# A decoder layer's projected keys: one copy out of PSUM as f32, both f16 halves made from that copy in SBUF

## What is computed

```python
q = qdq(x) @ qdq(wq).T + bq                    # 56 x 256 per batch, 16 heads of 16
kv = cond @ wkv.T + bkv                        # cond: 1500 x 256 per batch
k, v = jnp.split(kv, 2, axis=-1)
attn = softmax(einsum('bnhd,bmhd->bhnm', q, k) * scale)
o = einsum('bhnm,bmhd->bnhd', attn, v)
```

## Time and profile before

| what | value |
|---|---|
| median of 3 runs | 856.81 us (855.29 to 857.29) |
| the profiled execution | 855.01 us, of which 853.2 us are the span shown |
| TensorE busy | 772.5 us, 91% of the span |
| VectorE busy | 638.0 us, 75% |
| ScalarE busy | 510.9 us, 60% |
| GpSimd busy | 296.4 us, 35% |

### The profile page before, as it was taken

The page is one execution under the profiler, slowest core; times in us unless marked ns, Lnnn a source line. Parts: engine busy times, 40 slices in busy tenths (PEclk is TensorE's granted clock), DMA queues, the critical chain, the costliest instruction groups (busy, mean ns, idle before and its releaser), DMA issues.

```text
span 853.2 us, 30042 instructions
## 1 busy us (share of the span) xinstructions
PE 772.5 (91%) x12379; PEld 582.2 (68%) x12379; DVE 638.0 (75%) x1234; ACT 510.9 (60%) x1084; POOL 296.4 (35%) x366
## 2 busy tenths in 40 slices
PE   4689989999998999999899999999897799999996
PEld 2356666566666666666666666666665589999995
DVE  5877667777787879778787878877774735688887
ACT  2346666566576666666665666566654543777772
POOL 4263226232812461264217322722350003134232
PEclk9899999999999999999999999999999999999999
DMA  7366655454555556555555554645476975766653
GB/s 228 90 176 177 183 131 162 132 160 138 168 145 155 165 152 183 160 152 163 165 153 148 153 172 136 178 129 159 138 200 173 306 259 160 225 190 207 213 135 98
DMA packets 91380, 143.27 MB, mean 168 GB/s; under 512 B 11423, under 2 KB 79583, under 8 KB 87918
## 3 DMA queue, kind: packets, MB, share of 16 engines
q1 hardware_dynamic: 87742, 136.74, 53.8%
q0 software_dynamic: 3504, 4.62, 2.8%
HBM read 101.60 MB, written 39.68 MB: 166 GB/s over the span
## 4 chain that ended last, share of the span: by engine, by line
PE 62%; DVE 13%; ACT 10%; DMA 7%; issue 5%; SPq 2%; POOL 1%; DVEq 0%; POOLq 0%; ACTq 0%
PE ps L1655 14%; PE ps L1648 11%; PE ps L1967 7%; PE ps L1729 7%; PE ps L1707 6%; DVE negmax L522 4%; PE ps L2001 3%; DMA sums<-y_sb,g_token 3%; DMA k_st<-k_dram 3%; ACT pT L1437 3%; ACT k_front L1410 3%; PE ps L1671 3%; DVE k_front L516 3%; PE ps L1772 2%; PE ps L1988 2%
## 5 line engine op out<-in xcount | busy, mean ns | idle before, releaser
L522 DVE TENSOR_REDUCE negmax<-ps 112x1 f32<-112x1500 f32 x121 | 207.4, 1714 | 36.7 <-PE ps L1671 36.6
L1437 ACT ACTIVATE pT<-ps 125x448 f32<-125x448 f32 x384 | 195.6, 546 | 26.6 <-PE ps L1707 23.0
L1261 POOL TENSOR_TENSOR ctx_lo<-ctx_raw,ctx_hi 128x250 f16<-128x250 f32 x188 | 119.3, 666 | 177.8 <-DVE ctx_hi L507 177.8
L1707 PE MATMUL ps<-qbd,k_st 97*128 97x112 f16 x1536 | 128.2, 215 | 16.9 <-ACT pT L1437 8.9
L1707 PEld LDWEIGHTS ps<-qbd,k_st 97*128 97x128 f16 x1536 | 91.5, 99 | 73.1 <-ACT pT L1437 20.2
L1393 ACT COPY v_sb<-ps 125x512 f32<-125x512 f32 x96 | 56.3, 587 | 82.4 <-PE ps L1655 82.4
L516 DVE SCALAR_TENSOR_TENSOR k_front<-ps,bk_sb,k_front 128x500 f16<-128x500 f32 x80 | 58.8, 735 | 61.1 <-ACT k_front L1410 61.1
L1729 PE MATMUL ps<-pT,v_sb 125*17 125x56 f32 x6144 | 92.4, 216 | 8.5 <-issue 8.4
L1729 PEld LDWEIGHTS ps<-pT,v_sb 125*17 125x17 f32 x6144 | 80.6, 99 | 27.8 <-issue 16.1
L1410 ACT ACTIVATE k_front<-ps,bk_sb 128x500 f16<-128x500 f32 x80 | 54.3, 678 | 61.4 <-PE ps L1648 61.4
L1655 PE MATMUL ps<-wkv_hi,ctx_hi 128*125 128x256 f16 x384 | 76.4, 280 | 10.7 <-DVE k_front L516 9.2
(11 more groups left out here) (263 smaller groups left out, 1495.6 us busy)
## 6 DMA issues: line engine op xcount, KB each, us to landing
k_st<-k_dram SPq DMA_DIRECT2D x288, 125.0 KB, 3.0
w_sb<-w SPq DMA_DIRECT2D x25, 1024.0 KB, 5.0
ctx_raw<-ctx_T SPq DMA_DIRECT2D x48, 500.0 KB, 4.1
k_dram<-k_front SPq DMA_DIRECT2D x80, 250.0 KB, 2.7
xs<-zeros SPq DMA_DIRECT2D x28, 260.0 KB
w_sb<-w SPq DMA_DIRECT2D x8, 512.0 KB, 5.2
k_dram<-k_back SPq DMA_DIRECT2D x16, 250.0 KB, 2.9
xg<-xs SPq DMA_DIRECT2D x21, 130.0 KB, 4.1
```

The source lines that it names most:

```text
L522: V.tensor_reduce(negmax[0:QW], ps[0:QW, BANK_S:BANK_S + CHUNKS, 0:MC], AX.XY, ALU.max, negate=True).then_inc(max_done, 1)
L1261: last = nc.gpsimd.tensor_tensor(ctx_lo[:, k, c2, a], ctx_raw[:, k, c2, a], ctx_hi[:, k, c2, a], ALU.subtract)
L1437: nc.scalar.activation(pT[0:MT, (PAIRS * b + p) % 3, TPC * g:TPC * g + TPC], ps[0:MT, BANK_T + n % 2, 0:TPC * QW].rearrange("p (t n) -> p ...
L1707: last = mm(ps[:, BANK_T + n % 2, QW * i:QW * i + QW], k_st[:, j, p, a:a + P], qbd[:, j, p].rearrange("p h s -> p (h s)"), start=True, sto ...
```

## The change

A key unit now leaves PSUM once. ScalarE writes PSUM plus bias as f32 into one of two SBUF tiles (`k_full`) and counts `unit_out`. Then ScalarE, not VectorE, does a second instruction: it rounds that copy to f16 from SBUF (the high part). VectorE subtracts the high part from the f32 copy, both in SBUF, and counts a new semaphore `k_lo_done`, which the store waits for. There are four pairs of f16 tiles instead of six; ScalarE waits for the store of four key units ago, and for the low part of two key units ago. On SP, the load of unit 6 (the third block of group 0) moves from behind the store of unit 8 to behind the store of unit 6 itself.

```diff
@@ VectorE, unit_step
-                    dve.wait_ge(unit_done, UNITS * b + u + 1)
-                    dve.wait_ge(k_hi_done, len(KEY_UNITS) * b + KEY_UNITS.index(u) + 1)
-                    V.scalar_tensor_tensor(k_two[i][:, 1], ps[:, BANK_KV, 0:MC], bk_sb[:, g:g + 1], k_two[i][:, 0],
-                                           ALU.add, ALU.subtract).then_inc(unit_out, 1)
+                    n = key_number(b, u)
+                    dve.wait_ge(k_hi_done, n + 1)
+                    V.tensor_tensor(k_two[:, n % 4, 1], k_full[n % 2], k_two[:, n % 4, 0], ALU.subtract).then_inc(k_lo_done, 1)
@@ SP, store_keys and two_batches
-                sp.wait_ge(unit_out, UNITS * b + u + 1)
+                sp.wait_ge(k_lo_done, n + 1)
...
                         if u == 0:
                             load_keys(b - 1, j, KEY_UNITS[-1])
-                        else:
+                        elif u != 8:
                             load_keys(b, 1 - j, KEY_UNITS[KEY_UNITS.index(u) - 1])
+                        if u == 6:
+                            load_keys(b, 1 - j, u)
@@ ScalarE, k_hi_step
-                if b > 0:
-                    act.wait_ge(*stored(b - 1, u))
                 act.wait_ge(unit_done, UNITS * b + u + 1)
-                nc.scalar.activation(k_two[i][:, 0], ps[:, BANK_KV, 0:MC], ACT.Identity,
-                                     bias=bk_sb[:, g:g + 1]).then_inc(k_hi_done, 1)
+                if n >= 2:
+                    act.wait_ge(k_lo_done, n - 1)
+                nc.scalar.activation(k_full[n % 2], ps[:, BANK_KV, 0:MC], ACT.Identity, bias=bk_sb[:, g:g + 1]).then_inc(unit_out, 1)
+                if n >= 4:
+                    act.wait_ge(*stored(n - 4))
+                act.wait_ge(unit_out, UNITS * b + u + 1)
+                copy(k_two[:, n % 4, 0], k_full[n % 2]).then_inc(k_hi_done, 1)
```

More of the change, by code:

```diff
@@ L161, in decoder_layer @@
         wkv_lo = sb("wkv_lo", [P, CH, 2 * D], F16)
-        k_front = sb("k_front", [P, 5, 2, MC], F16)
+        k_two = sb("k_two", [P, 4, 2, MC], F16)
+        k_full0 = sb("k_full0", [P, MC])
         sb("behind_k_front", [P, 8], F32)
@@ L168, in decoder_layer @@
         k_st = sb("k_st", [KA, 2, PAIRS, M + 4], F16)
-        k_back = sb("k_back", [P, 2, MC], F16)
+        k_full1 = sb("k_full1", [P, MC])
         sb("behind_keys", [P, 616])
@@ L220, in decoder_layer @@
         b_oqT = a_t2[:, D:D + P].bitcast(BF16).rearrange("p (c n) -> p c n", c=CH)
-        k_two = [k_front[:, n] for n in range(5)] + [k_back]
+        k_full = [k_full0, k_full1]
         staging = pT[:].rearrange("p a m n -> p (a m n)")
@@ L273, in decoder_layer @@
         k_hi_done = sem("k_hi_done")
+        k_lo_done = sem("k_lo_done")
         unit_out = sem("unit_out")
@@ L434, in key_place, with key_number, stored @@
             return CH * c + g
-        def stored(b, u):
-            n = KEY_UNITS.index(u)
-            return k_out[n % 2], 16 * (len(KEY_UNITS) // 2 * b + n // 2 + 1)
+        def key_number(b, u):
+            return len(KEY_UNITS) * b + KEY_UNITS.index(u)
+        def stored(n):
+            return k_out[n % 2], 16 * (n // 2 + 1)
         def loaded(b):
@@ L511, in unit_step @@
                 if g in KEYS:
-                    i = key_place(c, g)
-                    dve.wait_ge(unit_done, UNITS * b + u + 1)
-                    dve.wait_ge(k_hi_done, len(KEY_UNITS) * b + KEY_UNITS.index(u) + 1)
-                    V.scalar_tensor_tensor(k_two[i][:, 1], ps[:, BANK_KV, 0:MC], bk_sb[:, g:g + 1], k_two[i][:, 0],
-                                           ALU.add, ALU.subtract).then_inc(unit_out, 1)
+                    n = key_number(b, u)
+                    dve.wait_ge(k_hi_done, n + 1)
+                    V.tensor_tensor(k_two[:, n % 4, 1], k_full[n % 2], k_two[:, n % 4, 0], ALU.subtract).then_inc(k_lo_done, 1)
             def max_step(b, p):
@@ L1082, in store_keys @@
                 c, g = UNIT[u]
-                i = key_place(c, g)
-                sp.wait_ge(unit_out, UNITS * b + u + 1)
+                i, n = key_place(c, g), key_number(b, u)
+                sp.wait_ge(k_lo_done, n + 1)
                 if not (isinstance(b, int) and b == 0):
                     sp.wait_ge(k_in[g], loaded(b - 1))
-                sp.dma_start(k_dram[i], k_two[i]).then_inc(stored(b, u)[0], 16)
+                sp.dma_start(k_dram[i], k_two[:, n % 4]).then_inc(stored(n)[0], 16)
                 for dst, src in between:
@@ L1094, in load_keys @@
                 i = key_place(c, g)
-                sp.wait_ge(*stored(b, u))
+                sp.wait_ge(*stored(key_number(b, u)))
                 for r, part in enumerate(KEY_PARTS[c]):
@@ L1173, in _ @@
                     load_keys(B - 2, 0, KEY_UNITS[-1])
-                else:
+                elif u != 8:
                     load_keys(B - 1, 1, KEY_UNITS[KEY_UNITS.index(u) - 1])
+                if u == 6:
+                    load_keys(B - 1, 1, u)
             load_keys(B - 1, 1, KEY_UNITS[-1])
```

## The result

The changed kernel takes 883.57 us (median of 4 runs, 881.98 to 885.50) against 857.05 in the runs beside it: a ratio of 1.0314, 95% interval 1.0286 to 1.0342. It is slower, as forecast, but by 26.5 us where 15.8 were forecast, and it lies 0.6 above the upper end of the range. The profiled execution took 882.58 us with a span of 880.8; that of before had 855.01 and 853.2.

A forecast was written before the change was run, and what follows sets the result against it. TensorE, busy 91%, was taken as the bound, so its longer waits are paid in full. 855.0 + 32.9 + 3.5 - 11.2 - 8.3 - 1.1 = 870.8; 1.8 to the median gives 872.6 us, range 854 to 883.

The forecast's parts named there:

- Borders: From even to odd slots, ScalarE's inserted cast delays TensorE's scores: 53 x 0.64 less 1.0, +32.9 us over the whole kernel.
- VectorE's chain: Slot 5: a later low part delays self-attention's maximum and subtraction, then ScalarE's exponential: 0.5 in seven batches, +3.5 us.
- Waits for VectorE: Value and key units no longer wait for VectorE's low part, as the bank is free after the read-out: -11.2 us.
- for loads: Scores find unit 6's keys there, since its load moves up by a slot: -8.3 us over the whole kernel.
- a rise by 1.1 from one stall less: Without the 4.5 us load wait before 656.80, the slowed matmuls and key unit behind it speed up: -1.1 us.
- The border's price: Cast of 0.61 us plus 0.03 wait on the f32 copy, between read-out and `qbd`: 0.64 us, bounds 0.60 and 0.67.
- the loads' -9.4: Unit 6's earlier load: 8.3 us of score waits and 1.1 of slowed TensorE work gone; bounds 0 and 9.4.
- the case in which the load doesn't help: Rival: SP stands at unit 6's store, all 9.4 us stay, 882.0 us; chance 0.09 together with VectorE meeting GpSimd.
- The faster one: Rival: the cast runs in ScalarE's idle time and only the early bank's and loads' gains count: 836.2 us; chance 0.13.
- No change: Rival: half of the borders hidden, gains as counted: -0.6, that is 856.2 us; chance 0.08.
- VectorE meeting GpSimd: Rival: a third of 96 low parts run 0.66 us longer beside GpSimd: +10.6, 883 us; chance 0.09 with the load case.

The follow-up runs named there:

- e9: The changed kernel once more, unchanged, for a second profile: 884.74 us (one run).
- e1: Changed kernel, but in even slots the cast stands behind the next odd slot's two exponentials, VectorE's low part behind its next row of maxima: 855.82 us.
- e2: Changed kernel, but VectorE, not ScalarE, casts the f32 copy to f16, directly ahead of its subtraction: 854.29 us.
- e5: e1, but SP issues the stores of units 5 and 6 one behind the other, with loads reordered around them: 850.31 us.
- e7: Kernel before the change with only the load of unit 6 moved behind its own store: 853.77 us.
- e12: e5, plus in the last batch the load of unit 8 behind its own store and the last expert weights behind the load of unit 11: 846.77 us.
- e11: Changed kernel, but from the fifth key unit on the cast makes only the first 250 of 500 columns: 872.11 us.
- e3: Kernel before the change plus a ScalarE cast of 500 unused f32 columns behind each high part, which nobody reads: 885.81 us.
- e6: Changed kernel, but the load of unit 6 stands behind the store of unit 8 again: 887.13 us.

## Why the prediction was wrong in size

The six iterations hold most of it, so here are its own terms for them. Borders 42 x 0.64 less 12 x 0.07: +26.0. VectorE's chain 6 x 0.5: +3.0. Waits for VectorE: -6.5, for loads -3.8. Together +18.7; measured +28.6, or 9.9 more.

- **The step that failed: there was no term for TensorE's clock.** The sum took the 1.00 of the earlier trace rows for granted, and a rise by 1.1 from one stall less. In its place the clock fell five times, and TensorE lost 8.5 us of full-clock work by it. The falls recurred in e9, five again, and in the six iterations the kernels without the cast at the borders (before, e1, e2, e5, e7, e12) have none or one, those with it 1 to 5. What they cost in time is less than 8.5. Slot 7 of the fifth iteration, from its `qbd` copy to the next one on ScalarE, is a place to read it, since the changed kernel has a fall there (first two rows) and e9, the same kernel, has none (last two):

```profile
509.87 0.24 ACT L1400 COPY qbd<-ps 1x112 f16<-1x112 f16 x1
...
515.73 0.24 ACT L1400 COPY qbd<-ps 1x112 f16<-1x112 f16 x1 [1.45 <-PE ps L1704]
...
512.01 0.24 ACT L1400 COPY qbd<-ps 1x112 f16<-1x112 f16 x1
...
516.26 0.24 ACT L1400 COPY qbd<-ps 1x112 f16<-1x112 f16 x1 [1.07 <-PE ps L1704]
```

5.86 us with the fall, 4.25 without (and 4.25 before the change): 1.6 more. In the first iteration the same slot takes 5.94 with a fall, but it did so before the change too, when TensorE waited there. Slot by slot beside the kernel before, the five falls add 0, 1.6, 1.2, 1.6 and 0.5: 4.9 of the 9.9. Over the whole span some of it is given back: the kernel before also has three falls in the last pair (from 656, 670 and 684 us), the changed one has one (from 698).
- **TensorE's busy time** goes with the falls: 448.7 to 451.0 without the cast at the border; with all of it 455.1 at one fall, 457.3 and 458.2 at three, 460.6 and 461.3 at four, 462.2 and 461.7 at five. Less 1.7 for each fall it is 448 to 450 without the cast and 452 to 455 with it. These 4 us are not the clock's, and they were not taken apart.
- **The border's price** came as forecast. The border from 12 to 13 got 0.64 longer on TensorE, and from one `shift_row` to the next the seven borders of an iteration cost 0.51 to 0.69 each and 4.3 together, where 7 x 0.64 less 2 x 0.07 = 4.3 were forecast. That the price is right is in part luck, because two errors cancel: the cast starts later than assumed, and the read-out earlier. e11 shows that every one of the seven pays the whole length.
- **VectorE's chain** exists: ScalarE's exponential waits for VectorE six times, 2.2 us in all. That is 0.37 each and not 0.5: -0.8.
- **Waits for VectorE and loads** went as forecast from the trace, but other waits came: those of `pv` for nothing visible went from 5.7 to 7.7 in the six iterations, +2.0. With the falls and the chain this makes 4.9 + 2.0 - 0.8 = 6.1 of the 9.9; the other 3.8 stay open. Nor was the loads' -9.4 a separate gain: e3 loses 6.3 of the 8.3 by longer slots alone, and e6 and e7 give 3.6 and 2.2 for the move, so the case in which the load doesn't help came true in good part. A wait that is taken away there lets TensorE run into the next one.
- **The preparation and first two batches** were to be even by the same terms (4.3 + 0.5 - 4.7) and lost 2.7. New waits there are 1.9 for the quantised tokens (0.6 before) and 1.2 of units for ScalarE's copy. They were not taken apart by a run.
- **The range** nearly held, by luck: its upper end stands for low parts of VectorE that run long beside GpSimd, or for a load that doesn't help, and not for the clock.
- **The rivals.** The faster one fell: the idle time of ScalarE does lie ahead of the read-out, and e11 shows no slack. When the cast alone is moved into that idle time (e1), the time is that of before; with the further moves on SP (e12) the rival comes true in part. No change fell with e11, where every border pays. VectorE meeting GpSimd is small, as follows.

The low part's durations in the changed kernel (count, ns min, median, max):

```profile
L520 DVE TENSOR_TENSOR k_two<-k_full,k_two x96: 672/680/1404, 13.5 to 690.5; 128x500 f16<-128x500 f32 x96
```

The median is 0.68, as estimated; some reach 1.40. The rule of the Trainium skill ("SBUF — State Buffer", Who interferes with whom), that a VectorE instruction with two SBUF inputs contends with GpSimd's reads, agrees with these few: all nine above 0.75 us ran while GpSimd made `q_mx` or `qbd`. Seven others that also ran beside `qbd`, for 0.6 us, took no more than 0.68. The mean is 0.735, so it is 96 x 0.055 = 5 us on VectorE in all, and TensorE has no wait for the low part in its list.

## What to carry to other kernels

Where an engine hands TensorE one small thing after another, count the places at which TensorE already waits for it, however short the waits are: at each of them a new instruction can cost its whole length, as at the seven borders here, and busy shares say nothing on it. Move such an instruction behind the hand-over, and then look at what is late next (here the stores). A sum of waits from a trace at full clock leaves out that a kernel with more short waits can run at a lower clock, and that a wait taken away can come back at the next place; give each a term of its own.

## What was not expected of the hardware

TensorE's granted clock fell to 1.2 GHz behind waits of 0.91 us and less: so it was in all eight falls at the border 6 to 7 in the two profiles of the changed kernel. One more fall in each came behind a wait of 1.49 for nothing visible. Each fall took 1.7 us of full-clock work, and slot 7 got up to 1.6 us longer. The Trainium skill ("TensorE: Matmul & The Clock Gate", A second HAM failure mode: psum-queue depth-cycling) tells of a kernel where "the PE micro-idles between MM groups frequently enough that HAM oscillates" (MM is a matmul, HAM the unit that grants the clock); the rows at 166.68 to 168.68 agree with it in that the waits are short. The waits alone do not decide: at four of these twelve borders, at 340.00 to 342.00 for one, the same waits were followed by no fall, nor did one follow any border 12 to 13, where TensorE waits as long (0.92).
